# A graph transformer and two graph convolutions in one pipeline: transposes moved in TensorE's order of work

## The reference

```python
scores = einsum('bhqd,bhkd->bhqk', q, k) / sqrt(HD) + beta * adj_e
scores = where(adj_e > 0, scores, -9e15)
out = einsum('bhqk,bhkd->bhqd', softmax(scores), v)
h = layernorm(x + out)
...
# each of the two inner layers
a = softmax(einsum('bid,bjd->bij', h, h) / sqrt(D))
delta = a * adjacency_matrix
attn = delta / (delta.sum(-1) + 1e-10)
hl, hs, hr = h @ wl.T + b_l, h @ ws.T + b_s, h @ wr.T + b_r
ctx = (attn * upper) @ hl + diag(attn) * hs + (attn * lower) @ hr
h = relu(layernorm(ctx) * g + beta)
...
x = layernorm(x + h)
```

## Time and profile before

| | us |
|---|---|
| median of 3 runs | 1282.96 |
| lowest and highest | 1282.18, 1283.35 |
| the profiled execution | 1282.98 |
| its span | 1281.2 |
| PE busy | 1263.4 |
| PEld busy | 1166.7 |
| DVE busy | 990.4 |
| ACT busy | 632.6 |
| POOL busy | 370.6 |

### The profile page before, as it was taken

How to read it: one execution, slowest core, us unless ns; L and a number is a source line. 1 busy time by engine, 2 the same in 40 slices (tenths; PEclk the granted TensorE clock), 3 DMA queues, 4 the chain that set the end, 5 groups by cost and what they waited for, 6 DMA issues and landing times.

```text
span 1281.2 us, 34717 instructions
## 1 busy us (share of the span) xinstructions
PE 1263.4 (99%) x13844; PEld 1166.7 (91%) x13844; DVE 990.4 (77%) x2691; ACT 632.6 (49%) x1338; POOL 370.6 (29%) x401
## 2 busy tenths in 40 slices
PE   9999999999999999999999999999999999999986
PEld 8999999999999999999999999999999999999975
DVE  6777778777878777787778787777877777877877
ACT  6544554544554445545445545455454455454543
POOL 3322323232323222323223232223232232323211
PEclk9999999999999999999999999999999999999989
DMA  8211110111110111110111101111101111011000
GB/s 275 85 39 57 58 57 25 35 57 57 57 57 4 55 57 57 57 28 31 57 58 58 57 15 44 57 57 57 43 16 57 57 58 58 20 39 45 26 14 26
DMA packets 53072, 66.34 MB, mean 52 GB/s; under 512 B 17840, under 2 KB 39856, under 8 KB 52784
## 3 DMA queue, kind: packets, MB, share of 16 engines
q1 hardware_dynamic: 52768, 63.93, 16.5%
q10 hardware_dynamic: 144, 0.20, 0.0%
HBM read 38.54 MB, written 12.58 MB: 40 GB/s over the span
## 4 chain that ended last, share of the span: by engine, by line
PE 97%; DVE 1%; issue 1%; ACT 1%; POOL 0%; POOLq 0%; DVEq 0%; ACTq 0%
PE bank L420 25%; PE bank L422 23%; PE bank L421 23%; PE bank L623 7%; PE bank L569 4%; PE bank L532 4%; PE bank L517 3%; PE bank L498 3%; PE bank L545 2%; PE bank L555 2%; PE bank L603 1%; PE bank L631 0%; DVE probs L1222 0%; POOL probs L1727 0%; PE bank L745 0%
## 5 line engine op out<-in xcount | busy, mean ns | idle before, releaser
L420 PE MATMUL bank<-w_hi,hT_hi 128*128 128x384 f32 x1158 | 405.4, 350 | 0.2 <-ACT hT_hi L1048 0.2
L422 PE MATMUL bank<-w_hi,hT_lo 128*128 128x384 f32 x1158 | 390.3, 337 | 0.0
L421 PE MATMUL bank<-w_lo,hT_hi 128*128 128x384 f32 x1158 | 390.1, 337 | 0.0
L420 PEld LDWEIGHTS bank<-w_hi,hT_hi 128*128 128x128 f32 x1158 | 218.3, 189 | 6.6 <-issue 2.0
L421 PEld LDWEIGHTS bank<-w_lo,hT_hi 128*128 128x128 f32 x1158 | 218.9, 189 | 0.0
L422 PEld LDWEIGHTS bank<-w_hi,hT_lo 128*128 128x128 f32 x1158 | 218.3, 189 | 0.0
L1293 DVE TENSOR_TENSOR hlr<-bank,rows 128x384 f32<-128x384 f32 x256 | 142.3, 557 | 70.9 <-PE bank L422 68.0
L1740 POOL TENSOR_TENSOR ln_rstd<-ln_var,minus_half 128x2 f32<-128x2 f32 x125 | 96.2, 769 | 322.1 <-DVE ln_var L1386 113.8
L1727 POOL TENSOR_TENSOR probs<-probs,row_max 128x768 f32<-128x768 f32 x64 | 94.6, 1478 | 265.7 <-DVE row_max L1228 265.7
L1310 DVE TENSOR_TENSOR late<-bank,rows 128x384 f32<-128x384 f32 x128 | 71.3, 558 | 118.0 <-PE bank L422 117.9
L420 PE MATMUL bank<-xT_hi,w_hi 128*128 128x256 f32 x558 | 158.7, 284 | 0.0
(11 more groups left out here) (131 smaller groups left out, 2370.9 us busy)
## 6 DMA issues: line engine op xcount, KB each, us to landing
v_halves<-v_stage SPq DMA_DIRECT2D x128, 99.0 KB, 2.3
x_in<-in_x SPq DMA_DIRECT2D x32, 384.0 KB, 4.0
xT_in<-in_xT SPq DMA_DIRECT2D x31, 384.0 KB, 3.4
out<-late SPq DMA_DIRECT2D x31, 384.0 KB, 2.4
late<-in_w SPq DMA_DIRECT2D x7, 576.0 KB, 6.5
adj_in<-in_adj SPq DMA_DIRECT2D x32, 96.0 KB, 3.8
adjT_in<-in_adjT SPq DMA_DIRECT2D x64, 48.0 KB, 3.2
rows<-in_vectors SPq DMA_DIRECT2D x1, 1536.0 KB, 8.7
```

The costliest lines, as they stand in the source:

```text
L420: nc.tensor.matmul(o, l_hi, r_hi, start=first and n == 0, stop=False)
L421: nc.tensor.matmul(o, l_hi, r_lo, start=False, stop=False)
L422: done = nc.tensor.matmul(o, l_lo, r_hi, start=False, stop=final and n == last)
```

## The change

It moves work in the orders of four engines, adds three waits and gives `transpose_probs` one in place of two; no instruction that computes is added or removed.

- PE, layer 0: `transpose_e` comes after both self parts, then `transpose_probs` follows at once (before, it came after `transpose_z`), then `mix`. Layer 1: `transpose_e` comes after the self part of tile 0, next to `transpose_h`.
- PE, waits: `transpose_probs` now waits for s_masked where it waited for v_staged and qk_ready; `project_v` waits for two copies of pT, `project_qk(0)` for all three, `attend` for v_staged.
- DVE: the row maxima come earlier, one between the sides of tile 0 and tile 1, the other behind the sides of tile 1; `mask_aT` of layer 0 comes after both self biases, that of layer 1 between them.
- ACT: the two exponentials come ahead of `scale_self` and `scale_turned`, and `take_pT` right behind these, ahead of `normalize_inner`.
- POOL: the second subtraction comes before the inverse root of the inner layer.

```diff
                     need(pe, s_masked, st.count(stage - 1, 4, 4))
                     need(pe, o_scaled, st.count(stage - 2, 2, 2))
+                    need(pe, pT_ready, st.count(stage - 1, 3, 2))
                 hi, lo = x_tiles(unit)
                 for t in range(T):
                     tok = slice(t * P, (t + 1) * P)
...
                 if unit >= 1:
                     need(pe, xhi_ready, st.count(EARLY, 1, 1))
                     need(pe, xlo_ready, st.count(EARLY, 1, 1))
+                if unit >= 2 and m == 0:
+                    need(pe, pT_ready, st.count(MID, 3, 3))
                 if unit == 1:
                     need(pe, s_masked, st.count(MID, 4, 4))
...
                     need(pe, v_staged, st.count(MID, 2, 1))
                 elif st.has(EARLY):
-                    need(pe, v_staged, st.count(EARLY, 2, 2))
-                    need(pe, qk_ready, st.count(EARLY, 6, 2))
+                    need(pe, s_masked, st.count(MID, 4, 4))
                 for t in range(T):
                     need(pe, p_ready, st.count(MID, 2, t + 1))
                     for j in range(PAIRS):
...
             def attend(st):
                 need(pe, v_moved, st.count(MID, 64, 64))
+                if st.has(EARLY) and st.unit(MID) > 0:
+                    need(pe, v_staged, st.count(EARLY, 2, 2))
                 for t in range(T):
                     need(pe, pT_ready, st.count(MID, 3, 2 + t))
                     o = O_BANKS[t][:, 0:H * VW].rearrange("p (h d) -> p h d", h=H)
...
                 if late:
                     gram(st, 0)
                     project_sides(st, 0)
-                    transpose_e(st, 0)
                     project_self(st, 0, 0)
                     project_self(st, 0, 1)
+                    transpose_e(st, 0)
+                if mid:
+                    transpose_probs(st)
+                if late:
                     mix(st, 0)
                 if early:
                     project_v(st, EARLY)
...
                     project_qk(st, 1)
                 if late:
                     transpose_z(st)
-                if mid:
-                    transpose_probs(st)
                 if early:
                     project_qk(st, 2)
                 if mid:
...
                 if late:
                     gram(st, 1)
                     project_sides(st, 1)
+                    project_self(st, 1, 0)
                     transpose_e(st, 1)
-                    project_self(st, 1, 0)
                 if mid:
                     transpose_h(st)
                 if late:
...
                     split_weight(7)
                     split_x(st)
                     split_weight(8)
-                    scale_self(st, 0)
-                    scale_turned(st, 0)
                 elif early:
                     split_x(st)
                 if late and st.unit(LATE) != 0:
                     exp_gram(st, 0)
+                if mid:
+                    exp_scores(st, 0)
+                if late:
                     scale_self(st, 0)
+                if mid:
+                    exp_scores(st, 1)
+                if late:
                     scale_turned(st, 0)
                 if mid:
-                    exp_scores(st, 0)
+                    take_pT(st)
                 if late:
                     normalize_inner(st)
-                if mid:
-                    exp_scores(st, 1)
                 if early:
                     take_qk(st, 0)
                     take_qk(st, 1)
                 if late:
                     take_zT(st)
-                if mid:
-                    take_pT(st)
-                if late:
                     split_zT(st)
                 if early:
                     take_qk(st, 2)
...
                     sides_bias(st, 0, 0, RIGHT)
                     if st.unit(LATE) == 0:
                         split_weight(6)
+                if mid:
+                    max_scores(st, 0)
+                if late:
                     sides_bias(st, 0, 1, LEFT)
                     if st.unit(LATE) == 0:
                         split_weight(7)
                     sides_bias(st, 0, 1, RIGHT)
-                    mask_aT(st, 0)
+                if mid:
+                    max_scores(st, 1)
+                if late:
                     if st.unit(LATE) == 0:
                         split_weight(8)
                     self_bias(st, 0)
-                if mid:
-                    max_scores(st, 0)
-                if late:
+                    mask_aT(st, 0)
                     make_ctx(st, LATE, 0)
                     stats_inner(st, LATE, 0, ln1_den, ln1_stats, ln1_aggr, ln1_eps, ln1_six, ln1_mv, ln1_var)
-                if mid:
-                    max_scores(st, 1)
                 if late:
                     shift(st, LATE, ln1_mv, ln1_rstd, ln1_shift, ln1_rs, ln1_sh)
                 if early:
...
                     shift(st, MID, ln0_mv, ln0_rstd, ln0_shift, ln0_rs, ln0_sh)
                 if late:
                     sides_bias(st, 1, 1, RIGHT)
+                    self_bias_tile(st, 1, 0)
                     mask_aT(st, 1)
-                    self_bias(st, 1)
+                    self_bias_tile(st, 1, 1)
                 if mid:
                     hT_low(st)
...
                     split_adj(st)
                 if mid:
                     shift_scores(st, 0)
+                    shift_scores(st, 1)
                 if late:
                     inverse_root(st, LATE, 1, 1, ln1_eps, ln1_var, ln1_rstd, ln1_rs)
-                if mid:
-                    shift_scores(st, 1)
                 if final:
                     inverse_root(st, FINAL, 1, 1, ln3_eps, ln3_var, ln3_rstd, ln3_rs)
                     inverse_root(st, FINAL, 1, 1, ln2_eps, ln2_var, ln2_rstd, ln2_rs)
```

More of the change, by code:

```diff
@@ L1113, in step @@
                 if late:
-                    normalize_inner(st)
+                    scale_self(st, 0)
                 if mid:
                     exp_scores(st, 1)
+                if late:
+                    scale_turned(st, 0)
+                if mid:
+                    take_pT(st)
+                if late:
+                    normalize_inner(st)
                 if early:
```

## The result

The changed kernel takes **1310.49 us** (median of 4 runs, 1310.08 to 1310.85), beside 1282.57 (1281.83 to 1283.35) of the kernel before on the same chip: 1.0219 times as long, 95% interval 1.0206 to 1.0233. The forecast was 1313.0, in a range of 1302 to 1321. The profiled execution spans 1308.3 us, 27.1 more than the 1281.2 before.

What follows compares the result with a forecast made beforehand. PE (TensorE) was taken as the bound, busy in all 39.04 us of a step. 29 steps x 0.89 = 25.8, plus 4 for the first, added to 1282.98 gave 1312.8, stated as 1313 us; range 1302 to 1321.

Steps and rivals of the forecast that it cites:

- The q/k wait: First product of project_qk(2): PE waits for ScalarE's copy of q and k, no longer covered by 12 transposes; 0.61 us a step.
- The late probabilities: Transposes of the probabilities before the mix: PE waits for the second tile's exponential; 0.25 us late a step.
- project_v's wait: First product of project_v: PE waits for two copies of take_pT, which stand behind scale_turned; 0.05 us more a step.
- rival 1: Only the wait at project_qk(2) bites, the chain of maxima being 0.3 us shorter; 1303 us, chance 0.12.
- Excursions: PE's switches from products to transposes and back: two fewer a step, one in each layer, gain 0.02 us.
- Rival 3: Faster: switches between products and transposes on PE cost more than the ends say; near 1272 us, chance 0.05.
- Rival 2: VectorE's second row maximum waits for POOL's first subtraction, 7 us more; 1320 us, chance 0.08.
- Rivals 1 and 4: The second named here: the waits are all hidden and the time stays at 1283 us, chance 0.05; rival 1 stands above.
- The first step: First inner step, with three weight splits on VectorE: mix near 50.3 instead of 45.03, about 4 us more, bounds 0 and 8.

Runs made afterwards that it cites:

- The own bank: The changed kernel with the third q/k projection in bank 1 instead of bank 2; 1293.6 us, 1.0085 times the kernel before.

## Why the prediction was right

- **The q/k wait**: forecast 0.61, measured 0.59, with the copy of k at the same distance and the reaction 0.14 where 0.15 was taken. The own bank took back 16.9 us, against 30 x 0.59 = 17.7, less 1.6 for the slower pace there: 16.1. What the Trainium skill's page (TensorE: Matmul & The Clock Gate, the table of specifications at its head) says of weight loads that are pulled ahead did not reach across this wait: the load came 0.11 behind the copy. The 0.5 that it would have given was the wrong number.
- **The late probabilities**: forecast 0.25, measured 0.17; this is the term that was mis-sized. Its chain was right: the second exponential ended 3.88 behind the last side product (606.96 after 603.08), reckoned 3.90. The end on PE was not. The reckoning gave 0.15 + 0.30 + 5 x 0.109 = 1.00 from there to the end of the six; they took 0.93. In the first step both tiles' waits can be seen: the first starts 0.15 behind its exponential (46.05 + 0.84, then 47.04), the second 0.05 (48.65 + 0.84, then 49.54). By the order shown above, the first waits for two semaphores and the second for one. The waits of PE read here fit that, but no run changed the number of semaphores alone, so the reason stays open. The 0.15 of the earlier trace rows was the wrong one of the two.
- **project_v's wait**: forecast 0.05, with the word that it sets the two together. Measured 0.03, and with the maxima sooner it was 0.10 of the 0.20: it hides half of that gain. The prediction's word that this path alone keeps the two at 0.30, which it also held against rival 1, was too strong: alone it costs 0.10.
- **Excursions**: forecast 0.02 a step, and by ends before rounding the stretch from the first side to the last self part is 0.012 us shorter in the first layer and 0.008 in the second. Rival 3, the faster one, falls with it: the kernel with the second layer's part alone and the one without waits show no more.
- **Rival 2**: the second maximum began at 603.58 beside POOL's subtraction (602.39 to 603.87) and took 0.94, as alone. It doesn't wait for POOL, and that rival falls. The Trainium skill's page that was named there (SBUF — State Buffer, Who interferes with whom) gives no lock to a VectorE instruction with one SBUF input outside a two-port mode, and the row agrees.
- **Rivals 1 and 4** fall with the two waits seen.
- **The first step**: forecast 4 and the mix near 50.3; measured 4.1 and 50.35. That the second exponential would end near 49.5, after scale_self, was right (49.49). VectorE's order did set the scaling: it waited for the self bias and ended at 47.97 + 0.62 = 48.59. What the working did not have is a second path that came out at the same time: POOL's two subtractions took 5.16 instead of 2.96 beside the splits and ended at 43.45 + 5.16 = 48.61. At their usual pace the exponential would still have stood behind scale_self and ended near 49.45 (an estimate: 48.59 + 0.02 + 0.84). That the two met within 0.02 us was luck; it is why the order tried for this step, which took scale_self out of the way, brought the exponential no sooner (POOL ended at 44.74 + 4.01 = 48.75 there).

**Sum**: 0.89 a step was forecast, 0.78 came (0.59 + 0.17 + 0.03 - 0.02 = 0.77 by the terms). 29 x 0.11 = 3.2 stands against the forecast's excess of 2.5 us over the median. So the mechanism was right, and no large errors cancelled.

## What to carry to other kernels

A move that brings like work together on the bounding engine is priced by the cover that it takes away: list which waits the moved work used to hide, and when the buffers behind them come free. Here two transposes next to others were worth nothing, and twelve taken from behind the z transposes laid bare a bank that was copied out 0.6 us too late. Read such waits by ends, since a pipelined engine's idle time shows only a part of them, and look at the first step of a pipeline apart: its extra work makes it another program.

## What had not been expected of the hardware

- **Two paces of one projection.** The third q/k projection ran at one of two paces, the same in nearly all steps of a kernel. PE in the changed kernel, and then in the one with the maxima first, each the first and the last of four products that are nine matmuls apart:

```profile
618.39 0.28 PE L420 MATMUL bank<-xT_hi,w_hi 128*128 128x256 f32 x1
...
619.42 0.28 PE L420 MATMUL bank<-xT_hi,w_hi 128*128 128x256 f32 x1
```

```profile
619.60 0.28 PE L420 MATMUL bank<-xT_hi,w_hi 128*128 128x256 f32 x1
...
620.66 0.28 PE L420 MATMUL bank<-xT_hi,w_hi 128*128 128x256 f32 x1
```

  1.03 / 9 is 0.114 us, 1.06 / 9 is 0.118. In their profiled executions the kernel before, the changed one, the changed one with z twice and the second layer alone have the first; all others have the second, which projections 0 and 1 have everywhere. The 18 matmuls are the same in all of them. It makes up to 2 us in 29 steps, as much as some of the terms here. What sets it stays open. Each kernel has one profiled execution, so whether the pace belongs to the kernel or to the execution is not shown either: of the changed kernel with z twice, the profiled run at the faster pace took 1310.85 and the three others 1312.97 to 1314.37.
- **A weight split on VectorE and a subtraction on POOL slow each other**: 2.02 instead of 1.34 for the split and 4.01 or 5.16 instead of 2.96 for the two subtractions. The one that began later lost: in the changed kernel each subtraction began just after a split and took 2.57 and 2.52, with the splits at 1.37 and 1.34; in the other order a split that began in a subtraction took the 2.02. The row maximum beside the same subtraction loses nothing.
- **The clock after a stall.** Two stalls of 1.5 to 2.5 us with six transposes between them went with the lower level (granted clock 0.50) for some 3 us in two kernels and some 7 in two others; in three with like stalls the clock stayed at 1.00. The price was 1.3 us in the mix alone (2.85 against 1.53).
